# Two 257-key cross-attentions: sums over values right behind the scores, the score keys between two halves of the turns, ScalarE's copy between exponentials

## What is computed

```python
# second layer (L1_xattn): x1 is the normalised x, x2 the context
q = (x1 @ Wq.T).reshape(B, N, H, D).transpose(0, 2, 1, 3)
k = (x2 @ Wk.T).reshape(B, M, H, D).transpose(0, 2, 1, 3)
v = (x2 @ Wv.T).reshape(B, M, H, D).transpose(0, 2, 1, 3)
q = _layernorm(q, ln_g, ln_b) * SCALE;  k = _layernorm(k, ln_g, ln_b)
attn = jax.nn.softmax(jnp.einsum('bhnd,bhmd->bhnm', q, k), axis=-1)
out = jnp.einsum('bhnm,bhmd->bhnd', attn, v)
return out.transpose(0, 2, 1, 3).reshape(B, N, C) @ Wp.T + bp
# third layer (L2_xattn): the same without the norms, with biases and a mask over the keys
scores = jnp.einsum('bhqd,bhkd->bhqk', Q, K) / jnp.sqrt(jnp.float32(DK))
scores = jnp.where(mask == 0, -jnp.inf, scores)
```

## Time and profile before

| | |
|---|---|
| time, median of 3 runs | 3612.77 us (3611.49 to 3614.55) |
| the profiled execution: its own time, its span | 3614.32 us, 3612.5 us |
| PE, DVE, ACT, POOL busy over the span | 83%, 69%, 56%, 52% |
| l1x_att: maxima of the first and of the last unit start at | 715.2 us and some 1110 us of the span |
| l2x_att: the same | 1641.1 us and some 2135 us |
| mean granted TensorE clock | 0.911 of 2.4 GHz |

### The profile page before, as it was taken

The page is one execution under the profiler, slowest core; times in us unless marked ns, Lnnn a source line. Parts: engine busy times, 40 slices in busy tenths (PEclk is TensorE's granted clock), DMA queues, the critical chain, the costliest instruction groups (busy, mean ns, idle before and its releaser), DMA issues. The chain is left out here.

```text
span 3612.5 us, 78060 instructions
## 1 busy us (share of the span) xinstructions
PE 3006.5 (83%) x23287; PEld 2034.0 (56%) x23287; DVE 2499.3 (69%) x7688; ACT 2030.6 (56%) x6297; POOL 1886.2 (52%) x2012
## 2 busy tenths in 40 slices
PE   6989698899998988678999987878772778969967
PEld 5769534477776866446666652333341446736645
DVE  7976677788887752447888876998976123457863
ACT  5545406699996543236777765454530124559954
POOL 5640203578886950445666657888850531117830
PEclk9999899899998999889999998989985888978989
DMA  3210003322220001111111114344440228900000
GB/s 107 89 33 0 6 1 92 115 85 85 86 86 30 1 7 56 39 50 38 34 34 34 34 33 141 136 140 136 134 148 14 33 41 239 210 8 2 2 7 23
DMA packets 142313, 233.86 MB, mean 65 GB/s; under 512 B 28652, under 2 KB 104718, under 8 KB 141431
## 3 DMA queue, kind: packets, MB, share of 16 engines
q1 hardware_dynamic: 133944, 221.59, 20.7%
q0 software_dynamic: 8128, 9.45, 1.5%
HBM read 200.42 MB, written 13.71 MB: 59 GB/s over the span
## 5 line engine op out<-in xcount | busy, mean ns | idle before, releaser
L3239 PE MATMUL l2a_pY<-l2a_hc,ident 128*128 128x512 f32 x512 | 275.2, 676 | 89.5 <-POOL l2a_hc L3158 55.3
L2488 POOL TENSOR_TENSOR l2x_att_prob<-l2x_att_prob,l2x_att_rs 128x1024 f32<-128x1024 f32 x128 | 242.3, 1893 | 170.2 <-DVE l2x_att_rs L2707 170.2
L3128 POOL TENSOR_TENSOR l2a_dbu<-l2a_dx,l2a_BC 128x1024 f32<-128x1024 f32 x128 | 298.5, 2352 | 21.0 <-PE l2a_pY L3239 10.7
L2488 POOL TENSOR_TENSOR l1x_att_prob<-l1x_att_prob,l1x_att_rs 128x1024 f32<-128x1024 f32 x128 | 242.3, 1893 | 81.2 <-DVE l1x_att_rs L2707 78.1
L3256 ACT ACTIVATE l2a_pA<-l2a_dl,l2a_A 128x512 f32<-128x512 f32 x256 | 174.5, 689 | 188.1 <-DVE l2a_pH L3362 112.8
L2660 ACT ACTIVATE l2x_att_prob<-l2x_att_prob,l2x_att_nmx 128x257 f32<-128x257 f32 x512 | 252.8, 499 | 1.3 <-DVE l2x_att_nmx L2702 1.3
L2660 ACT ACTIVATE l1x_att_prob<-l1x_att_prob,l1x_att_nmx 128x257 f32<-128x257 f32 x512 | 252.9, 499 | 0.7 <-DVE l1x_att_nmx L2702 0.6
L3239 PEld LDWEIGHTS l2a_pY<-l2a_hc,ident 128*128 128x128 f32 x512 | 103.9, 212 | 252.4 <-issue 120.2
L3362 DVE TENSOR_TENSOR_SCAN l2a_pH<-l2a_pA,l2a_dbu 128x512 f32<-128x512 f32 x192 | 224.8, 1217 | 23.3 <-POOL l2a_dbu L3128 12.2
L2702 DVE CUSTOM_DVE_ANT_0 l2x_att_prob<-l2x_att_pS,l2x_att_mask 128x257 f32<-128x257 f32 x512 | 187.4, 423 | 28.1 <-PE l2x_att_pS L2578 27.8
L2702 DVE CUSTOM_DVE_ANT_0 l1x_att_prob<-l1x_att_pS,l1x_att_mask 128x257 f32<-128x257 f32 x512 | 186.5, 421 | 4.0 <-PE l1x_att_pS L2578 3.8
(11 more groups left out here) (765 smaller groups left out, 9009.3 us busy)
## 6 DMA issues: line engine op xcount, KB each, us to landing
l2a_BC<-l2a_rows SPq DMA_DIRECT2D x128, 512.0 KB, 3.8
l3x_att_ctn<-ctx_n SPq DMA_DIRECT2D x32, 576.0 KB, 12.2
l0x_att_kvs<-ctx_t SPq DMA_DIRECT2D x32, 514.0 KB, 3.5
l1x_k_xin<-ctx_t SPq DMA_DIRECT2D x32, 514.0 KB, 3.5
l1x_att_ctx<-ctx_t SPq DMA_DIRECT2D x128, 128.5 KB, 2.1
l1x_att_kT<-l1x_KA SPq DMA_DIRECT2D x128, 128.5 KB, 2.1
l2x_att_ctx<-ctx_t SPq DMA_DIRECT2D x128, 128.5 KB, 2.1
l3x_att_ctx<-ctx_t SPq DMA_DIRECT2D x32, 514.0 KB, 10.2
```

Of the source, the lines that this page charges most:

```text
L2488: pool.tensor_tensor(p, p, bc(rs[:, b, :], 2, LAST), ALU.mult).then_inc(scaled, 1)
L3128: pool.tensor_tensor(dbu[:, u % 3], dx[:, g % 2], bc(BC[:, u % RING, 0, :], 1, NC), ALU.mult).then_inc(dbu_made, 1)
L3239: last = pe.matmul(pY[c][:, :], env.ident[:, :], hc[:, u % 3, c, :], start=False, stop=n == NS - 1)
```

## The change

The change reorders calls on three engines; no instruction is added or removed but the semaphore's registers around them, and the work is the same.

- TensorE: in a slot, `attend(n - 2)` (with `turn_tails` and `output`) comes right behind `scores(n + 1)`, before the turns of n-1; in l2x_att the key product stands between `turn(n - 1, .., 1)` and `turn(n - 1, .., 0)`.
- ScalarE: its copy of the turned half stands between the exponentials of the head groups 0, 1 and those of 2, 3.
- VectorE: two maxima, the factors, two maxima; then the key copy and `keep_turned`; then `keep_tails` or `add`; and `own_head` directly before `sum_heads`.

```diff
 # TensorE
                 def slot(n, c, k):
                     if inside(n + 1):
                         scores(n + 1, c, k)
-                    if inside(n - 1):
-                        turn(n - 1, (c - 1) % 4, 1)
-                        turn(n - 1, (c - 1) % 4, 0)
                     if c == 1 and inside(n - 5):
                         pe.wait_ge(tail_kept, made(2 * (k - 1) + 1))
                     if inside(n - 2):
...
                     if c == 2 and inside(n - 6):
                         output(k - 1)
+                    if inside(n - 1):
+                        turn(n - 1, (c - 1) % 4, 1)
                     if inside(n + 2) and KA is None:
                         keys(n + 2, c, k)
+                    if inside(n - 1):
+                        turn(n - 1, (c - 1) % 4, 0)
 # ScalarE
                 def slot(n, c, k):
+                    if inside(n + 1):
+                        exponentials(n + 1, (c + 1) % 4, (0, 1))
                     if inside(n - 1):
                         keep_turned(n - 1, (c - 1) % 4)
                     if inside(n + 1):
-                        exponentials(n + 1, (c + 1) % 4)
+                        exponentials(n + 1, (c + 1) % 4, (2, 3))
 # VectorE
                 def slot(n, c, k):
+                    if inside(n + 1):
+                        maxima(n + 1, (c + 1) % 4, k if c < 3 else k + 1, (0, 1))
                     if inside(n):
                         factors(n, c)
                     if inside(n + 1):
-                        maxima(n + 1, (c + 1) % 4, k if c < 3 else k + 1)
-                    if inside(n - 2):
-                        own_head(n - 2, (c - 2) % 4, k if c >= 2 else k - 1)
+                        maxima(n + 1, (c + 1) % 4, k if c < 3 else k + 1, (2, 3))
+                    if inside(n + 2) and KA is None:
+                        keys(n + 2, c)
+                    if inside(n - 1):
+                        keep_turned(n - 1, (c - 1) % 4)
                     if c == 1 and inside(n - 5):
                         keep_tails(k - 1)
                     if c == 2 and inside(n - 6):
                         add(k - 1)
-                    if inside(n + 2) and KA is None:
-                        keys(n + 2, c)
-                    if inside(n - 1):
-                        keep_turned(n - 1, (c - 1) % 4)
+                    if inside(n - 2):
+                        own_head(n - 2, (c - 2) % 4, k if c >= 2 else k - 1)
                     if inside(n - 2):
                         sum_heads(n - 2, (c - 2) % 4)
```

More of the change, by code:

```diff
@@ L2655, in last_keys, with exponentials @@
                     act.activation(mt[:, :], M, ACT.Copy).then_inc(mo_kept, 1)
-                def exponentials(n, b):
-                    for j in range(R):
+                def exponentials(n, b, heads):
+                    for j in heads:
                         act.wait_ge(m_made, made(R * n + j))
@@ L2661, in exponentials @@
                                               bias=nmx[:, b, j:j + 1], scale=-1.0, accum_out=sums[:, b, j:j + 1])
-                    last.then_inc(p_made, 1)
+                    if heads[-1] == R - 1:
+                        last.then_inc(p_made, 1)
                 def keep_turned(n, b):
@@ L2694, in _, with maxima @@
                     dve.wait_ge(mask_made, 1)
[L2696 to L2701, removed]
+                def maxima(n, b, k, heads):
+                    if heads[0] == 0:
+                        after(dve, t_made, 2 * (n - 4) + 1)
+                        after(dve, tail_kept, 2 * (k - 1) + (b == 3))
+                        dve.wait_ge(s_made, made(n))
+                    for j in heads:
                         dve.tensor_tensor_reduce(prob[:, b, j, 0:KEYS], pS[:, j, 0:KEYS], mask[:, :], -1.0, BIG,
```

## The result

The changed kernel takes 3570.4 us (median of 4 runs, 3564.4 to 3576.8), the kernel before 3613.7 us beside it: a ratio of 0.9863, 95% interval 0.9839 to 0.9887. Timed a second time it is 3567.1 us against 3618.2, ratio 0.9851 (0.9824 to 0.9879). It is faster, as forecast, but by 43 to 51 us and not by 18. The median lies on the very edge of the range, and well outside the forecast's own range of 3587 to 3604; the gain is more than twice the one forecast.

The account below looks back on a forecast made before the run. PE bounds l1x_att; its wait for VectorE's key copy bounds l2x_att. A 9.9 us loss and a 28.2 us gain make -18.3 from 3614.3: 3596.0, median 3595 us; 8-in-10 range 3570 to 3617, forecast's own 3587 to 3604.

Parts of the forecast that it names:

- The bound and the wait that goes: PE full in l1x_att; in l2x_att its wait for VectorE's key copy goes, with 0.09 us to spare.
- What is late next: own_head, now behind VectorE's copy of the second half, holds the next slot's `attend` in both stages.
- way back: From own_head's end on VectorE to PE's `attend`: 0.24 us, the loop's value, taken for every slot.
- What PE's order costs by itself: PE's steps summed in the new order: 2.79 us a slot in l1x_att, 3.23 in l2x_att.
- the surcharge of a turn: Extra time on PE for a turn behind matmuls using part of the array: 0.07 us, between nothing and 0.10.
- plain slot: Slot of PE's scores, sums, both half turns and values: 2.79 us in l1x_att, 3.23 with keys in l2x_att.
- the circle: `attend`, half turns, VectorE's copy, own_head, back to `attend`: 2.89 us in l1x_att, 3.39 in l2x_att at c = 3.
- my rival sum of 4 us more: If scores to sums on PE also drains: 0.07 us more in one slot of four, 4 us in both stages.
- ScalarE's edit costs nothing and gives nothing: ScalarE's copy between the exponentials: no cost or gain by itself, as `attend` needs that copy only a slot later.
- The second case: Way from turn to own_head and back some 0.10 us shorter per slot: 3575 us, l1x_att unchanged; chance 0.22.
- The third: VectorE's copy starts 0.70 instead of 0.64 us behind a half turn: 11.5 us more, 3606; chance 0.18.
- The slower one: Turns pay the full 0.10 us and a half takes 0.51: +8.7 us against before, 3621; chance 0.15.

Follow-up runs that it names:

- TensorE's order alone: Kernel before with only TensorE's new order, VectorE and ScalarE keeping the old one: 3628.7 us, ratio 1.0023.
- two bare orders: The change plus 12 slots of TensorE's work alone in the old order and 12 in the new, ahead of l1x_att: 3636.8 us, one run.
- the better version: The change with own_head and the kept tails or addition ahead of VectorE's copy of the second half: 3543.5 us, ratio 0.9777; again 3545.0 us.

## Why the prediction was right and wrong

**The bound and the wait that goes: right.** The key copy was what PE waited for; the wait is gone in the change, most of it is gone in TensorE's order alone (7.1 us of 24.7 are left), and it is back, with the whole loss, when the keys go behind both turns. The margin was 0.09 us by my steps and is 0.05 by the measured ones (1.42 us of PE's work against the 1.37 of the key copy's way): 1803.86 needed no wait.

**"What is late next": right in kind, too long by its way back.** own_head is what PE waits for in c = 1 and c = 2, and putting it ahead of the copy removes the wait and 20 us of the stages. The links were measured at 0.64, 0.60 and own_head's 0.34, as forecast. The last link, the way back to PE, was not: I took 0.24 us everywhere. Measured are, at the `attend` that ends the slot, 0.15 in c = 1 (own_head's end at 1804.66, `attend` at 1804.81), 0.26 in c = 2 (1808.24 + 0.34 to 1808.84), and in c = 3 at most 0.06 in l2x_att (1811.93 to 1811.99) and 0.10 in l1x_att (854.82 to 854.92). These distances are the same, within 0.02, in nearly all of some 25 slots of each kind. Why they differ from slot to slot I did not find out. The `attend` that ends c = 2 has one wait more in the kernel than the others, for the addition, and that was not tested.

**"What PE's order costs by itself": the other step that failed.** I took 0.07 us for the surcharge of a turn behind the scores, by the row of the keys, and carried the same surcharge over to a turn behind the sums. With one surcharge for both, the two halves take 1.02 or 1.03 us in either order, whatever its size; this is why my plain slot came to 2.79 us. In the changed trace a half turn without a surcharge takes 0.44 us (1802.88 to 1803.32), so two take 0.88. The surcharge behind the scores was then 1.02 - 0.88 = 0.14 us, outside my bounds of nothing to 0.10, but behind the sums it is only 0.05 (0.93 - 0.88; the first half 0.49 behind the tails and 0.50 behind the sums), and behind the output nothing. A plain slot is 2.69 us in l1x_att and 3.14 in l2x_att (3.15 measured), not 2.79 and 3.23. The two bare orders show that this price is the order's own, without any wait.

By slots, from `attend` to `attend`:

| | l1x_att forecast, measured | l2x_att forecast, measured |
|---|---|---|
| c = 3 | 2.89, 2.69 | 3.39, 3.15 |
| c = 0 | 3.01, 2.91 | 3.45, 3.35 |
| c = 1 | 3.27, 3.13 | 3.77, 3.63 |
| c = 2 | 3.56, 3.55 | 4.06, 4.03 |
| sum | 12.73, 12.28 | 14.67, 14.16 |

The 0.45 and 0.51 us per round are 14 and 16 us, 31 in all; the time was off by 25, since some 6 us came back outside the stages. About half of the 31 belongs to each of the two steps:

- c = 0: all 0.10 us are the cheaper order.
- c = 1: 0.06 are the first half turn (0.49 for 0.55) and 0.09 the way back.
- c = 3: my 2.89 and 3.39 were the circle's, not PE's own work. The first half turn gives 0.06 of it, the way back 0.14 in l1x_att and 0.18 in l2x_att. With the way back of 0.24 the circle would still have lasted 2.83 and 3.33 us, and with my PE order PE's own work 2.79 and 3.23; it took both.
- c = 2: right to 0.03.

TensorEngine Tiling (Array Packing), section Key Properties, in the Trainium skill says that a change of the tiling mode drains TensorE. The changes from part to whole agree with it, at 0.05 to 0.14 us each, but they do not cost alike. I also counted by the rule wrongly: a plain slot of the old order has four changes of mode and one of the new order three, so by the rule the order saves one, not nothing. That is the way the runs went, and my rival sum of 4 us more was wrong. What the change from scores to sums costs no run here can tell, since the sums stand behind another mode in both orders, at 0.57 us behind the turns and behind the scores.

**"ScalarE's edit costs nothing and gives nothing": wrong in l1x_att.** It gives 0.32 us per round there and 0.23 in the better version, 10 and 7 us; in l2x_att nothing, as said. I had looked at who waits for the copy, and not at what stands behind it in ScalarE's queue: the exponentials, which the factors and GpSimd's scaling need, and the copy of the values, which PE's last keys need. The place of the factors, which I had only priced as a cost that is "mostly covered", is worth 19 us in the changed kernel. So the l1x_att that I took to be bound by PE alone was a balance of four engines at 80 to 100% each; TensorE's order by itself cost it 36 us.

**The rivals.** The second case, a way back some 0.10 us shorter, was true in good part: over the three slots with a circle the way back was in the mean at least 0.08 us shorter than I took (0.15, 0.26 and at most 0.06 in l2x_att). Its sign, an unchanged l1x_att, came too: 12.28 for 12.42. Its sums for c = 1, 3.17 and 3.67, come near the 3.13 and 3.63 measured, those for c = 2, 3.46 and 3.96, do not (3.55 and 4.03). But its 3575 us lie near the 3570 measured in part by luck: its rounds of 12.43 and 14.37 leave out the cheaper order, which gave another 0.15 and 0.21, 11.5 us, and some 6 us came back outside. The third (a copy 0.06 later) did not happen. The slower one joined a full surcharge of 0.10 to a half turn of 0.51, which cannot both be: with 1.02 us for both halves a larger surcharge leaves a cheaper half, 0.46. The slower side exists, though, and is reached without ScalarE's and VectorE's part: 3628.7 us.

**Open.** Why the way back to PE has its own length in each kind of slot. What makes the unchanged rest of the program vary by up to 25 us between profiled executions, by which some 6 to 13 us of the stages' gain are missing from their times, though not from the second timing's median (51 us). Whether it is VectorE's copy that still holds `attend` in the better version, where in l2x_att a round is 13.96 us and PE's own work by the steps above 4 x 3.14 + 0.22 + 0.19 + 0.49 = 13.46: the delays of `attend` behind that copy, 0.55 us, have the right size, but no run moved the copy.

## What to carry to other kernels

Price an order of matmuls by its neighbours: look in the trace for the same matmul behind each kind of neighbour, and if a pair is not there, measure the bare sequence before summing. When a move takes an instruction's cover, list the whole queue of each engine behind the instruction that waits; an edit on an engine that "costs nothing" can be what keeps the next circle from closing. A price measured behind one neighbour does not hold behind another: the surcharge of a turn was 0.14 us behind the scores and 0.05 behind the sums. And when a new wait shows, ask which instruction stands ahead of the releaser without need: own_head needed only the sums over values, and putting it ahead of a 0.6 us copy made the two stages another 20 us shorter, beside the 49 of the change.

## What the runs showed of the hardware

- Fp32 transposes of the whole array (eight, 0.88 us behind whole-array products) took 0.14 us more behind matmuls of 32 rows (1.02) and 0.05 more behind matmuls of 32 columns (0.93). The values, products of the whole array, took 0.11 more behind matmuls of 32 columns (0.65 for 0.54). The sums, of 32 columns, took 0.57 behind matmuls of 32 rows as behind whole-array transposes.
- The release from VectorE to TensorE, from the end of own_head to the start of `attend`, was 0.15 us in c = 1 and 0.26 in c = 2, and at most 0.06 in c = 3 of l2x_att, each the same round after round. With own_head ahead of the copy, a delayed `attend` started 0.10 or 0.19 us behind the copy's end.
